# Attention scores of two heads in two 64-row tiles of TensorE, with the diagonal corrections on TensorE and a plain max on VectorE

## What is computed

```python
q, k, v = x @ wq.T, x @ wk.T, x @ wv.T           # split into 16 heads of 8
attn = q @ k.T / sqrt(8) - slope[h] * abs(i - j)  # 256 x 256 per head
attn = softmax(attn)
out  = attn @ v                                   # heads joined: 256 x 128
x1   = layernorm(x + out @ wo.T + bo)
```

## Time and profile before

| | |
|---|---|
| median of 3 runs | 962.63 us (962.04 to 964.39) |
| the profiled execution | span 961.6 us from the first instruction to the last, 1.0 us less than the median of the runs |
| attention | from the start to about 592 us |
| feed-forward | from about 597 us to the end |
| busy | TensorE 95%, VectorE 77%, ScalarE 68%, GpSimd 15% |

### The profile page before, as it was taken

One profiled execution on the slowest core, in us unless ns is written; L12 is line 12 of the kernel. 1 busy time (PEld: TensorE's weight loads), 2 busy tenths in 40 slices (PEclk: granted clock), 3 DMA queues, 4 the chain that ended last, 5 costly groups with the idle time before them and its releaser, 6 DMA issues. The chain is left out here.

```text
span 961.6 us, 24138 instructions
## 1 busy us (share of the span) xinstructions
PE 911.5 (95%) x6914; PEld 724.1 (75%) x6914; DVE 737.4 (77%) x3039; ACT 654.9 (68%) x1168; POOL 140.6 (15%) x213
## 2 busy tenths in 40 slices
PE   1899999999999999999999996899999999999995
PEld 1677778787787877878778774688888888888883
DVE  5789898888888888888888873667766777776764
ACT  4277676676666766667666764677777777777773
POOL 3002112121211212112121132000010000000101
PEclk9799999999999999999999998899999999999998
DMA  6244443444434344443444420001111111111001
GB/s 176 79 134 114 129 116 109 125 107 129 114 111 126 105 125 117 113 122 106 126 118 116 124 80 20 25 25 45 33 33 33 33 44 42 34 39 37 23 23 44
DMA packets 72307, 80.60 MB, mean 84 GB/s; under 512 B 8208, under 2 KB 68368, under 8 KB 69200
## 3 DMA queue, kind: packets, MB, share of 16 engines
q1 hardware_dynamic: 71392, 77.28, 28.9%
q0 software_dynamic: 880, 2.88, 1.1%
HBM read 45.53 MB, written 33.55 MB: 82 GB/s over the span
## 5 line engine op out<-in xcount | busy, mean ns | idle before, releaser
L614 DVE CUSTOM_DVE_ANT_0 scored<-ps_a,corner_rows 128x256 f32<-128x256 f32 x1024 | 376.1, 418 | 21.7 <-PE ps_a L371 8.6
L524 ACT ACTIVATE probs<-ps_b 128x512 f32<-128x512 f32 x512 | 301.7, 599 | 128.7 <-PE ps_b L362 125.8
L371 PE MATMUL ps_a<-qk_stack 126*128 126x256 f32 x1024 | 255.4, 333 | 17.2 <-DMA qk_stack<-qk_scratch 15.1
L383 PE MATMUL ps_b<-qk_stack 128*128 128x256 f32 x1024 | 209.5, 286 | 2.3 <-ACT probs L524 2.1
L371 PEld LDWEIGHTS ps_a<-qk_stack 126*128 126x128 f32 x1024 | 162.3, 197 | 47.1 <-issue 29.7
L383 PEld LDWEIGHTS ps_b<-qk_stack 128*128 128x128 f32 x1024 | 159.3, 191 | 6.5 <-ACT probs L524 3.8
L848 ACT ACTIVATE gelu_f<-ps_r,sc 128x512 f32<-128x512 f32 x128 | 88.3, 690 | 79.9 <-PE ps_r L789 72.4
L396 PE MATMUL ps_o<-probs,v_aug 128*32 128x256 f32 x2048 | 137.0, 385 | 0.4 <-ACT probs L524 0.4
L362 PE MATMUL ps_b<-corner_sb,idb_sb 128*128 128x158 bf16 x512 | 125.3, 245 | 0.0
L786 PE MATMUL ps_r<-g1h,h_hi 128*128 128x512 f32 x256 | 102.6, 401 | 2.0 <-DVE g1l L913 1.9
L786 PE MATMUL ps_r<-g2h,h_hi 128*128 128x512 f32 x256 | 102.8, 401 | 0.0
(11 more groups left out here) (99 smaller groups left out, 1366.8 us busy)
## 6 DMA issues: line engine op xcount, KB each, us to landing
qk_stack<-qk_scratch SPq DMA_DIRECT2D x64, 384.0 KB
qk_scratch<-x_parts SPq DMA_DIRECT2D x32, 512.0 KB, 3.0
qk_scratch<-x_parts SPq DMA_DIRECT2D x32, 256.0 KB, 3.3
xT_sb<-in_xT SPq DMA_DIRECT2D x32, 128.0 KB, 2.1
x_sb<-in_x SPq DMA_DIRECT2D x32, 128.0 KB, 2.1
x_scratch<-x_sb SPq DMA_DIRECT2D x32, 128.0 KB, 1.7
x_in<-x_scratch SPq DMA_DIRECT2D x32, 128.0 KB, 2.1
x_res<-x_scratch SPq DMA_DIRECT2D x32, 128.0 KB, 2.1
```

What stands on the lines that cost most here:

```text
L371: mm = pe.matmul(ps[:, qb * SEQ:(qb + 1) * SEQ], q_stack[par][0:KA, h, qb * P:(qb + 1) * P], k_stack[par][0:KA, h, :], start=(qb == 0), st ...
L383: pe.matmul(ps[:, kb * SEQ:(kb + 1) * SEQ], k_stack[par][:, h, kb * P:(kb + 1) * P], q_stack[par][:, h, :], start=(kb == 0), stop=False, s ...
L524: nc.scalar.activation(probs[:, k % HALF, :], ps_b[k % 2][:], ACT.Exp, scale=slope[k]).then_inc(exp_done, 1)
L614: ins = nc.vector.tensor_tensor_reduce(scored[:, k % 2, qb, :], ps_a[A_BANK[k]][:, qb * SEQ:(qb + 1) * SEQ], corner_rows[:, qb, :], -1.0, ...
```

## The change

**Layout.** The 16 heads are put in two groups, even and odd ones. `qk_stack` holds 8 heads in partitions 0 to 63 and 8 in partitions 64 to 127. Per head there are 24 rows of features and 4 for the bias, with rows of zeros A contracts over 33 (`KA`), and B over two more that hold the maximum (`KB` = 35). What the bias rows don't make is added by matmuls on the diagonal blocks of 64 x 64.

**Scores.** For each `k`, A of head `k` and B of head `k ^ 1` are issued in turns; one is in the upper 64 rows of the array and the other in the lower. Each is two float32r matmuls of 256 columns and two bf16 corrections of 128 columns. The waits of both stand ahead of all eight.

**VectorE** takes the maximum of a bank with one plain `tensor_reduce` over 128 x 2 x 256.

**The order.** All other work of TensorE is put in four places, next to the four PV products (`k` = 1, 5, 9, 13). The output part of a batch is done one step later, so the loop has one step more at its end. The scale of the queries is put into the weight once, so that high parts and low parts of queries and keys take one instruction each.

```diff
-PE_AT = {"last pv": 1, "turn max 1": 1, "v": 2, "qk": 4, "turn o 0": 6, "turn o 1": 7, "turn max 0": 9, "turn norm": 10, "wo": 12}
-ACT_AT = {"max hi 1": 1, "copy o 1": 2, "v": 3, "qk hi": 4, "max hi 0": 9, "oT": 10, "copy o 0": 11}
-DVE_AT = {"max lo 1": 1, "qk lo": 4, "norm": (7, 8), "max lo 0": 10, "res": 13, "stats": 14}
+PE_AT = {"last pv": 1, "turn max 1": 1, "wo": 1, "qk": 5, "turn o 0": 5, "turn max 0": 9, "turn o 1": 9, "v": 13, "turn norm": 13}
+ACT_AT = {"max hi 1": 1, "copy o 1": 2, "qk hi": 6, "max hi 0": 9, "copy o 0": 10, "v": 13, "oT": 14}
+DVE_AT = {"max lo 1": 2, "res": 3, "stats": 4, "qk lo": 6, "norm": (7, 11), "max lo 0": 10}
...
-        qk_stack = [sb(f"qk_stack{i}", [P, 2, HEADS, SEQ], F32R) for i in range(2)]
+        qk_stack = [sb(f"qk_stack{i}", [P, 2, HG, SEQ], F32R) for i in range(2)]
...
+            def score_max(b, par, h, qb):
+
+                g, j = h % GROUPS, h // GROUPS
+                rows_of = slice(g * TILE, g * TILE + KA)
+                pe.matmul(ps_a[A_BANK[h]][:, qb * SEQ:(qb + 1) * SEQ], q_stack[par][rows_of, j, qb * P:(qb + 1) * P],
+                          k_stack[par][rows_of, j, :], start=(qb == 0), stop=False, skip_group_check=True)
...
+            def add_corner(ps, g, turned, sub):
+
+                rows_of = slice(g * TILE, (g + 1) * TILE)
+                out = ps[:].rearrange("p (b c) -> p b c", c=P)[:, 0:4:3, sub * TILE:(sub + 1) * TILE]
+                return pe.matmul(out, eye_sb[rows_of, sub, :], corner_sb[rows_of, 2 * turned + sub, :, :], start=False,
+                                 stop=True, skip_group_check=True)
+
+            def scores(t, s, k):
+
+                in_a, in_b = live(t + 1, BATCH), live(t, BATCH)
+                if in_a:
+                    if k % HALF == 0:
+                        wait(pe, stacked[k // HALF], (t + 2) * GROUPS * DMA)
+                    wait(pe, max_done, a_released(t + 1, k))
+                if in_b:
+                    if k % HALF == 0:
+                        wait(pe, m_landed[k // HALF], (t + 1) * 2 * GROUPS * DMA)
+                    wait(pe, exp_done, t * HEADS + k - 1)
+                for half in range(BLK):
+                    if in_a:
+                        score_max(t + 1, 1 - s, k, half)
+                    if in_b:
+                        score_exp(t, s, k, half)
+                for sub in range(2):
+                    if in_a:
+                        mm_a = add_corner(ps_a[A_BANK[k]], k % GROUPS, 0, sub)
+                    if in_b:
+                        mm_b = add_corner(ps_b[k % 2], (k ^ 1) % GROUPS, 1, sub)
+                if in_a:
+                    mm_a.then_inc(scores_a, 1)
+                if in_b:
+                    mm_b.then_inc(scores_b, 1)
...
-                        for qb in range(BLK):
-                            ins = nc.vector.tensor_tensor_reduce(
-                                scored[:, k % 2, qb, :], ps_a[A_BANK[k]][:, qb * SEQ:(qb + 1) * SEQ], corner_rows[:, qb, :], -1.0, F32_MAX,
-                                ALU.add, ALU.min, negmax[:, k // HALF, k % HALF, qb:qb + 1])
-                        ins.then_inc(max_done, 1)
+                        nc.vector.tensor_reduce(negmax[:, k // HALF, k % GROUPS, k % HALF // GROUPS, :],
+                                                ps_a[A_BANK[k]][:].rearrange("p (b k) -> p b k", b=BLK),
+                                                AX_X, ALU.max, negate=True).then_inc(max_done, 1)
```

More of the change, by code:

```diff
@@ L60 @@
 STACK = 3 * DH
-MROW = P - 2
-KA = MROW
-STEPS_T = (MROW - STACK - 4) // BLK
-CORNER = P - STEPS_T
-F32_MAX = float(np.finfo(np.float32).max)
+GROUPS = 2
+TILE = P // GROUPS
+HG = HEADS // GROUPS
+HH = HG // 2
+KA = 33
+MROW = KA
+KB = KA + 2
 QH, QL, KH, KL = range(4)
@@ L289, in stack @@
             def stack(b, par, hf):
-                heads = slice(hf * HALF, (hf + 1) * HALF)
-                sp.dma_start(qk_stack[par][0:STACK, :, heads, :].bitcast(F32),
-                             qk_dram[par, :, :, :, heads, :].rearrange("n r d h t -> (r d) n h t")).then_inc(stacked[hf], DMA)
+                half = slice(hf * HH * SEQ, (hf + 1) * HH * SEQ)
+                src = qk_dram[par].rearrange("n r d (g j) t -> g (r d) n (j t)", g=GROUPS)
+                for g in range(GROUPS):
+                    dst = qk_stack[par][g * TILE:g * TILE + STACK, :, :, :].bitcast(F32).rearrange("p n j t -> p n (j t)")
+                    sp.dma_start(dst[:, :, half], src[g, :, :, half]).then_inc(stacked[hf], DMA)
             def spill(par):
@@ L475, in step @@
                         mm.then_inc(oT_done, 1)
-                    if k == PE_AT["turn max 0"] and live(t + 1, BATCH):
-                        if live(t - 1, BATCH):
-                            wait(pe, normed, (t - 1) * 2 + 1)
-                        else:
-                            wait(pe, qk_lo, (t + 2) * 2 + 2)
-                        turn_max(t + 1, 0)
-                    if k == PE_AT["wo"] and live(t - 1, BATCH):
-                        wait(pe, oT_copied, t)
-                        for qb in range(BLK):
-                            mm = pe.matmul(ps_m[1][:, qb * D:(qb + 1) * D], oT_sb[:, qb * P:(qb + 1) * P], wo_sb[:],
-                                           start=True, stop=True)
-                        mm.then_inc(wo_done, 1)
+                    if k in PV_AT and live(t, BATCH):
+                        pv(t, s, PV_AT.index(k))
+                    if k == PE_AT["last pv"] and live(t - 1, BATCH):
+                        pv(t - 1, 1 - s, 3)
             drive(pe, step, **STEPS)
@@ new lines, in step @@
+                    if k == DVE_AT["stats"] and live(t - 2, BATCH):
+                        wait_apart(dve, bn_done, (t - 1) * BLK, passed["dve"])
+                        for a in range(BLK):
+                            nc.vector.bn_aggr(meanvar[s][:, a, :], bn6[:, a, :]).then_inc(stats_done, 1)
+                    if k == DVE_AT["qk lo"] and live(t + 2, BATCH):
+                        wait(dve, qk_hi, t + 3)
+                        nc.vector.tensor_tensor(qk_sb[:, QL:KL + 1:KH, :], ps_m[0][:].rearrange("p (n t) -> p n t", n=2),
+                                                qk_sb[:, QH:KL:KH, :].bitcast(F32), ALU.subtract).then_inc(qk_lo, 1)
```

294 lines of the change are left out of this document (128 added, 166 removed).

## The result

| | before | after |
|---|---|---|
| median | 963.41 us (962.04 to 964.39, 4 runs) | 1126.24 us (1123.78 to 1147.16, 4 runs) |
| ratio | | **1.1698** (1.1661 to 1.1736) |
| span of the profiled execution | 961.6 us | 1126.6 us |
| mean granted clock over the span | 0.983 | 0.912 |

What follows compares the result with a forecast made beforehand. TensorE, busy 95%, was taken as the bound at 17.13 us a step. New step 6.6 + 8.4 + 4.2 + 0.85 = 20.05 us; 961.6 + 90.5 - 3 + 3, plus 1.0, gave 1053 us, range 1000 to 1130 us.

Steps and rivals of the forecast that it cites:

- walk: Timing four heads in a row through TensorE and ScalarE: waits of 1.11 us a run, three times, and 0.91 in the fourth.
- full-clock step: One attention step after the change was forecast at 20.05 us, 2.92 more than 17.13, times 31 steps: +90.5 us.
- Heads: A and B of a head on TensorE, side by side: 0.41 us a head, 6.6 us a step instead of 9.6.
- no side by side: Rival: the pairs of score matmuls take turns on TensorE, 0.72 us a head, 1130 us in all; chance 0.13.
- Round trip waits: B needs the exponential of two heads before; third and fourth heads of each run of four wait, 4.2 us a step.
- the run with `oT`: Fourth run (heads 14, 15, 0, 1), whose ScalarE copy is half as long: fourth head waits 0.39 us, the run 0.91.
- VectorE at `k` = 9: Low parts delay the maxima's transpose and `turn_o`: 0.5 and 0.35 us a step, between 0 and 1.2.
- other work and changes of shape: TensorE's work between heads, 7.53 us, plus four more tile-shape changes at 0.2 us: 8.4 us a step, 7.5 as lower bound.
- VectorE's plain maximum: A 512-element reduction per head takes about 0.59 us back to back, 9.4 us a step; its gain is hidden.
- Start and end: Outside the full steps: start -3 us (-6 to 0) from halved fills, end +3 us (0 to 6) from the extra step.
- The clock falls: Rival: gaps lower TensorE's granted clock to 1.2 GHz, its work about doubles, beyond 1300 us; chance 0.04.
- Late DMAs: More DMA issues for half stacks and maximum rows, costed at nothing; without cover, each late landing would hold head 0 or 8.

Runs made afterwards that it cites:

- 9: Changed kernel with B of head k in place of head k^1, so A and B share one half of the array: 1316.88 us, ratio 1.3672.
- 4: Kernel before with one plain maximum per head on VectorE, the corner additions to A left out: 961.30 us, ratio 0.9984.
- 12: Kernel before, full-height scores, with B of every head waiting for the exponential of the head just before it: 1156.57 us, ratio 1.2042.
- 8: Changed kernel with the product with `wo` moved from beside PV to behind the second head of a run of four: 1115.52 us, ratio 1.1561.
- 7: Changed kernel with all of A's matmuls of a head issued first, then all of B's, under the same joint wait: 1120.60 us, ratio 1.1677.
- 2: Changed kernel with A's first matmul issued three more times ahead of the exponential wait at third and fourth heads of a run: 1086.36 us, ratio 1.1298.

## Why the prediction was right and wrong

**Direction and walk: right.** The full-clock step is 19.94 us for 20.05.
- Heads: 0.44 us for 0.41, 0.5 us a step more. The waits for `probs` came out 0.5 us less; that these cancel is luck, and the two terms are each right to about a tenth. Pairs start together, and the rival "no side by side" falls: 9 shows what that looks like.
- Round trip waits: third head 0.47 us for 0.52, fourth 0.52 to 0.57 for 0.59, the run with `oT` 0.68 for 0.91 (and 0.2 us more that no bracket shows, since its fourth head starts 0.64 us behind the third); 3.70 a step for 4.2.
- VectorE at `k` = 9: 0.38 and 0.48 us for 0.5 and 0.35, 0.86 for 0.85.
- What is left is 19.94 - 16 x 0.44 - 4.56 = 8.34 us of other work and changes of shape, for 8.4. It is a remainder: the 0.2 us for coming out of a PV is in no line of the earlier trace rows, and no run isolates it.
- VectorE's plain maximum: 340.9 us for 512 on the page after, 0.67 each where I had 0.59; its gain was hidden (4), as forecast.

**Start and end: small.** I had -3 and +3; measured +0.9 and +5.9, so the start has the wrong sign. The fills of the stack did halve (3.8 and 2.4 us busy in the first 60 us for 7.5 and 4.6), and the start is no shorter; why is not settled.

**The clock: wrong, and it is most of the 71 us.** The step that failed is the rival "The clock falls", which got 0.04 and a price beyond 1300 us. I treated it as all or nothing, 1.2 GHz for the whole attention, and dismissed it since the gaps are short and the slices of the feed-forward with small gaps keep 9. The chip did neither: it lowered the clock in most steps, each for a part, so that the three steps from 469 to 537 us shown above cost 1.6 to 3.7 us more. And the evidence I dismissed it with came from full-height matmuls, which 12 shows to bear pauses that 64-row tiles don't. I also misread that row where I argued for the rival: TensorE waits most in the first slice, whose clock digit is 9, and the lower digit, 7, belongs to the second, where it is busy at eight tenths. The measured 1126 us lies inside my range by luck: only because that reached to a rival, "no side by side", which was not what happened.

**Late DMAs: put at nothing.** I wrote that each late landing would hold head 0 or 8 and priced none. That is what the loads at 127.84 and 406.29 show: 8.3 us of waits over the steps, of which some 4 to 8 are lost by the estimate above.

The Trainium skill ("TensorE: Matmul & The Clock Gate", A second HAM failure mode: psum-queue depth-cycling) describes a kernel in which frequent short idle moments between groups of matmuls make the clock go back and forth between its levels. The trace after agrees: 0.66 to 1.00 from step to step, and no wait over 0.68 us in the step at 426 us. Run 12 narrows it: as much idle time under full-height matmuls gave 0.98.

**Why it is slower at all.** TensorE was the bound at 17.13 us a step and lost 2.6 us of scores (16 x 0.60 to 16 x 0.44). Then the bound became the round trip of a head through ScalarE, which shorter heads cannot shorten: the saving turned into waits of 4.56 us, and the other work took about 0.8 us more, which I put to the changes of tile shape. That makes 19.94 us; the rest is the clock and, for a few us in all, the late DMAs.

## What to carry to other kernels

When an engine is the bound at 95%, ask of each saving what the next head would wait for, and walk the round trip with the queue of the other engine in it: that gave the full-clock step within 1%, with two terms off by 0.5 us that cancelled. Price a landing that has only a few microseconds of cover. Of TensorE's clock, ask two things together: does the change bring pauses, and does it also make each matmul use fewer rows; with both, price a step that loses clock for a part of its time, not a clock that is either whole or halved. If single products are at hand, put them into the pauses instead of beside PV (8: 0.45 us a step).

## What the runs showed of the hardware

- Two 64-row tiles run side by side: eight matmuls (four of 256 columns of float32r, four of 128 of bf16) take 0.44 us a head as pairs, and in one tile the heads start 0.60 us apart, their float32r matmuls 0.12 us (9).
- The halves go their own way. In 7, B's first matmul starts 0.01 us behind A's first and 0.33 us ahead of A's first correction, although it stands behind all of A in the program. The Trainium skill ("TensorEngine Tiling (Array Packing)", Key Properties) says that tiles work independently, and the trace agrees. The Trainium skill ("TensorE: Matmul & The Clock Gate", The mechanism) has matmuls start in program order, and across the two halves this trace does not.
- TensorE's granted clock can be low while the profile shows it busy: 0.74 at 98% busy with one half-height tile at a time (9), 0.98 at 87% busy with full height (12). Neither "busy" nor the idle time alone tells the clock.
- Adding 24 matmuls a step made a kernel 40 us faster (2).
- Behind an idle time of 2.94 us for a DMA, TensorE ran at the lower level for the 13 us from 127.5 to 140.5 (clock 0.50), busy for 12.62 of them (after).
